# ALiBi attention: the distance bias of the diagonal blocks for heads 2 to 15 as factors on the exponentials, multiplied in by GpSimd, in place of TensorE products

## The reference, cut to what matters

```python
dist = jnp.abs(pos[:, None] - pos[None, :])
bias = -dist[None, :, :] * slopes[:, None, None]          # slopes = 0.5 ** head
scores = jnp.einsum('bhid,bhjd->bhij', q, k) / scale + bias
attn = jax.nn.softmax(scores, axis=-1)
out = jnp.einsum('bhij,bhjd->bhid', attn, v)
```

## Time and profile before

| | |
|---|---|
| time, median of 3 runs | 2564.29 us (2558.7 to 2565.91) |
| the profiled execution, its own time | 2567.91 us |
| its span in the trace | 2566.0 us |
| PE busy | 2248.5 us (88%) |
| DVE busy | 1718.1 us (67%) |
| ACT busy | 1463.6 us (57%) |
| POOL busy | 1089.2 us (42%) |
| granted TensorE clock, mean | 0.953 of full speed |

### The profile page before, as it was taken

One profiled execution on the slowest core, in us unless ns is written; L12 is line 12 of the kernel. 1 busy time (PEld: TensorE's weight loads), 2 busy tenths in 40 slices (PEclk: granted clock), 3 DMA queues, 4 the chain that ended last, 5 costly groups with the idle time before them and its releaser, 6 DMA issues. The chain is left out here.

```text
span 2566.0 us, 52577 instructions
## 1 busy us (share of the span) xinstructions
PE 2248.5 (88%) x21574; PEld 1674.9 (65%) x21574; DVE 1718.1 (67%) x2800; ACT 1463.6 (57%) x2382; POOL 1089.2 (42%) x800
## 2 busy tenths in 40 slices
PE   2799999999999779999879999999999985878476
PEld 1577777777777556666547777777777753766276
DVE  3677777777788457777467777778878845533554
ACT  0467676666666425555547767676666643435342
POOL 4655556555565100000065655556556505410432
PEclk8899999999999879999879999999999987999898
DMA  7000000099999300000000000000000012210013
GB/s 148 1 1 1 2 2 2 1 94 114 107 102 117 25 1 2 2 2 2 1 1 2 2 1 2 1 2 1 2 2 2 1 52 64 57 51 1 32 53 96
DMA packets 185425, 73.63 MB, mean 29 GB/s; under 512 B 79658, under 2 KB 181204, under 8 KB 185060
## 3 DMA queue, kind: packets, MB, share of 16 engines
q1 hardware_dynamic: 177172, 56.68, 19.0%
q0 software_dynamic: 5568, 10.12, 1.3%
q10 hardware_dynamic: 2448, 3.48, 0.6%
HBM read 24.05 MB, written 46.18 MB: 27 GB/s over the span
## 5 line engine op out<-in xcount | busy, mean ns | idle before, releaser
L467 POOL TENSOR_TENSOR work<-work,rot_tables 128x512 f32<-128x512 f32 x256 | 446.5, 1764 | 443.7 <-ACT work L566 443.7
L475 POOL TENSOR_TENSOR work<-work 128x1024 f32<-128x1024 f32 x128 | 305.1, 2383 | 13.0 <-DVE work L885 3.1
L885 DVE TENSOR_TENSOR work<-work,rot_tables 128x1024 f32<-128x1024 f32 x128 | 162.2, 1267 | 112.1 <-ACT work L566 112.1
L1042 DVE TENSOR_REDUCE small<-psum 128x4 f32<-128x1024 f32 x128 | 156.5, 1223 | 92.5 <-PE psum L1550 92.4
L1276 PE MATMUL psum<-qkv_w_hi,h_hi 128*128 128x512 f32 x384 | 182.6, 476 | 18.9 <-POOL h_lo L494 16.4
L1430 PE MATMUL psum<-centered,ffn_w 128*128 128x256 f32 x768 | 190.4, 399 | 6.1 <-DVE centered L946 2.9
L902 DVE TENSOR_TENSOR work<-work,small 128x1024 f32<-128x1024 f32 x128 | 159.5, 1248 | 51.2 <-ACT small L580 47.0
L677 ACT ACTIVATE work<-psum 128x1024 f32<-128x1024 f32 x128 | 131.2, 1025 | 102.3 <-PE psum L1557 102.3
L1368 PE MATMUL psum<-work 64*128 64x128 f32 (+1 forms) x2048 | 181.1, 307 | 0.0
L482 POOL TENSOR_TENSOR y_all<-centered,squared 64x256 f32<-64x256 f32 x64 | 48.5, 759 | 296.2 <-ACT squared L626 293.6
L1430 PEld LDWEIGHTS psum<-centered,ffn_w 128*128 128x128 f32 x768 | 145.8, 196 | 36.3 <-DVE centered L946 17.7
(11 more groups left out here) (280 smaller groups left out, 5561.5 us busy)
## 6 DMA issues: line engine op xcount, KB each, us to landing
h_area<-mean_weights SPq DMA_DIRECT2D x16, 2048.0 KB
tile_x<-h_area SPq DMA_DIRECT2D x78, 64.5 KB, 1.9
work<-y_tokens SPq DMA_DIRECT2D x8, 512.0 KB, 6.2
stage<-in_consts ACTq DMA_DIRECT2D x1, 3009.0 KB, 12.7
work<-in_x SPq DMA_DIRECT2D x4, 512.0 KB, 28.4
expert_w<-in_ew SPq DMA_DIRECT2D x1, 2048.0 KB, 8.5
expert_w<-in_ew SPq DMA_DIRECT2D x8, 256.0 KB, 6.8
out<-work SPq DMA_DIRECT2D x8, 256.0 KB, 3.5
```

The costliest lines, as they stand in the source:

```text
L467: last = pool.tensor_tensor(b[:, :, :, o_], a[:, :, :, i_], tab[:, l, 1, t, :, o_].unsqueeze(2).to_broadcast([P, 2, HEADS, 32]), ALU.mult)
L475: pool.tensor_tensor(rC[:, t, :], rC[:, t, :], rB[:, t, :], ALU.add).then_inc(f_sum, 1)
L885: dve.tensor_tensor(g(rC[:, t, :]), g(rA[:, t, :]), tab[:, l, 0, t, :, :].unsqueeze(2).to_broadcast([P, 2, HEADS, DH]), ALU.mult)\
L1042: dve.tensor_reduce(dst, PS[:, 0:2, :].rearrange("p b (t j) -> p b t j", t=TILES), AX, ALU.max, negate=True).then_inc(a_smax, 1)
```

## The change

For the pairs `r = 1` to `7` (heads 2 to 15) the four bias products behind the turned scores are gone; pair 0 keeps them, and the plain scores keep them for all pairs. In their place GpSimd multiplies the exponentials of the two diagonal blocks by exp(-2 * slope * relu(distance)), a product of 128 partitions by 512 elements in place in `PT4`, seven for each sequence (`far`). ScalarE makes the factors once, at the beginning of the layer, in the tile `y_all`, which the ffn stages use and which is free then: 14 activations of 128x256. `attend` now waits for GpSimd too (`a_f`), and on TensorE it is moved by one slot, from the odd to the even ones; `o_out` moves with it on ScalarE, from slots 3 and 7 to slots 4 and 0. `PT4` has three buffers in place of two. On GpSimd `split_h` is now written in the slot loop, in slot 5 behind that slot's `far`.

```diff
-        PT4 = [work[0][:, 2048 * n:2048 * (n + 1)].rearrange("p (h i) -> p h i", h=4) for n in range(2)]
+        PT4 = [work[0][:, 2048 * n:2048 * (n + 1)].rearrange("p (h i) -> p h i", h=4) for n in range(3)]
+        fac = Y[:, :, 1:T + 1].rearrange("p h (t i) -> p h t i", t=TILES)
...
+                def far(u):
+                    h, w = 2 * (u % 8), 2 * (u % 2)
+                    pool.wait_ge(a_p, u + 1)
+                    e = PT4[u // 2 % 3][:, w:w + 2, :].rearrange("p h (q i) -> p h q i", q=4)[:, :, 0:4:3, :]
+                    pool.tensor_tensor(e, e, fac[:, h:h + 2, :, :], ALU.mult).then_inc(a_f, 1)
+
+                pool.wait_ge(a_fac, 1)
+                for k in range(-2, SEQS + 4):
+                    for p in range(8):
+                        u = 8 * k + p - 11
+                        if 0 <= u < 8 * SEQS and u % 8:
+                            far(u)
+                        if p == 5 and k + 2 < SEQS:
+                            split_h(k + 2)
...
+                act.wait_ge(x_done, SEQS)
+                for h in range(2, AH):
+                    last = act.activation(fac[:, h, :, :], relub[:, :, :], ACT.Exp, scale=-2.0 * 0.5 ** h)
+                last.then_inc(a_fac, 1)
...
-                        if p == 3 and 0 <= k - 2 < SEQS:
+                        if p == 4 and 0 <= k - 2 < SEQS:
                             o_out(k - 2, 1)
-                        if p == 7 and 0 <= k - 1 < SEQS:
-                            o_out(k - 1, 0)
+                        if p == 0 and 0 <= k - 2 < SEQS:
+                            o_out(k - 2, 0)
...
+                    if turned and r > 0:
+                        far.then_inc(a_st, 1)
...
-                    if turned:
+                    if turned and r == 0:
...
                     pe.wait_ge(a_p, 2 * w + 2)
+                    pe.wait_ge(a_f, 7 * k + 2 * c + 1)
...
-                        if u % 2 == 0 and 0 <= (u - 2) // 2 < 4 * SEQS:
-                            attend((u - 2) // 2)
+                        if u % 2 == 1 and 0 <= (u - 3) // 2 < 4 * SEQS:
+                            attend((u - 3) // 2)
```

More of the change, by code:

```diff
@@ L305, in build @@
             ("zero", "mean", "centered", "squared", "var", "rstd", "normed", "h_split", "qk", "qk_hi", "qk_split")]
-        a_v, a_vs, a_s, a_smax, a_m, a_mT, a_madd, a_st, a_p, a_o, a_oTs = [sem(f"attn_{n}") for n in
-            ("v", "v_sb", "s", "s_max", "m_split", "mT", "m_added", "st", "p", "o", "oT_sb")]
+        a_v, a_vs, a_s, a_smax, a_m, a_mT, a_madd, a_st, a_p, a_f, a_fac, a_o, a_oTs = [sem(f"attn_{n}") for n in
+            ("v", "v_sb", "s", "s_max", "m_split", "mT", "m_added", "st", "p", "p_far", "factors", "o", "oT_sb")]
         a_rows, a_on, a_oT, a_ocs, a_proj = [sem(f"attn_{n}") for n in
@@ L514, in attn, with split_h @@
                     pool.memset(Vs[n][:, :, :, ADH:ADH + 1], 1.0).then_inc(a_zero, 1)
-                for n in range(SEQS):
+                def split_h(n):
                     pool.wait_ge(a_norm, n + 1)
@@ L676, in exps @@
                     act.wait_ge(a_st, u + 1)
-                    act.activation(PT4[u // 2 % 2][:, 2 * (u % 2):2 * (u % 2) + 2, :], PS[:, 4:6, :], ACT.Exp)\
+                    act.activation(PT4[u // 2 % 3][:, 2 * (u % 2):2 * (u % 2) + 2, :], PS[:, 4:6, :], ACT.Exp)\
                         .then_inc(a_p, 1)
@@ L1543, in scores @@
                             for b in range(2):
-                                pe.matmul(PS[:, 4 + b, t * T:(t + 1) * T], ks[m % 3][row(r, b), r // 2, t * P:(t + 1) * P],
-                                          qs[m % 3][row(r, b), r // 2, :], start=t == 0, stop=False, skip_group_check=True)
+                                far = pe.matmul(PS[:, 4 + b, t * T:(t + 1) * T], ks[m % 3][row(r, b), r // 2, t * P:(t + 1) * P],
+                                                qs[m % 3][row(r, b), r // 2, :], start=t == 0, stop=r > 0,
+                                                skip_group_check=True)
+                    if turned and r > 0:
+                        far.then_inc(a_st, 1)
                     if plain:
@@ L1569, in attend @@
                             last = pe.matmul(PS[SLOT * h:SLOT * (h + 1), 6, (c % 2) * T:(c % 2 + 1) * T],
-                                             Vs[k % 3][:, j, 4 * c + h, :], PT4[w % 2][:, h, j * T:(j + 1) * T],
+                                             Vs[k % 3][:, j, 4 * c + h, :], PT4[w % 3][:, h, j * T:(j + 1) * T],
                                              start=c % 2 == 0 and j == 0, stop=j == 1, skip_group_check=True)
```

## The result

The changed kernel takes 2596.06 us (median of 4 runs, 2594.89 to 2597.55) against 2562.82 us: a ratio of 1.0137, interval 1.0116 to 1.0158. It is 33 us slower, where 22 were forecast. The profiled execution took 2595.75 us with a span of 2593.9.

A forecast was written before the change was run, and what follows sets the result against it. TensorE was taken as the bound, busy 40.68 of 43 us, with VectorE's loop close behind. 20.4 + 1.3 + 0.3, +0.5 at the start, -0.5 at the end gave +22: 2590 profiled, 2586 median; own range 2574 to 2598.

The forecast's parts named there:

- a pitch of +2.4: Upper case per sequence, against +1.7 forecast: restarts behind the reduction at 0.14 us in place of 0.05.
- What is moved: `attend`, 1.00 us of TensorE, goes from odd slots to slots 0, 2, 4 and 6: +1.7 us, 23.1 us a sequence.
- the saving comes through: Rival, 11%: TensorE's work alone counts, 1.64 us a sequence saved, 2542 us; TensorE idle below 1 us a sequence.
- The loop over the reduction: Scores, VectorE's reduction, next scores: a slot cannot be shorter than this, 2.16 us, however little TensorE has to do.
- The restart of 0.05: TensorE starts the next scores 0.05 us after VectorE's reduction ends.
- give almost nothing: Removing the turned biases in a slot that a loop bounds: the slot goes from 2.26 to 2.16 us.
- What is added: GpSimd's products, taken at 1.4 us each, latency hidden; 14 activations for factors at the start, 0.5 us uncovered.
- Twelve sequences have the whole pattern: Sum over the layer: 12 x 1.7 = 20.4 us, plus 1.3 for the sequence ahead and 0.3 for the last.
- The end: End of the layer: ScalarE's loop gains 2 us, the last `attend` waits +1.2 to 1.8; taken as -0.5 us.
- The beginning: Start of the layer: the factors' activations, mostly beside GpSimd's memsets that hold back `center`; taken as 0.5 us.
- the first rival: 15%: TensorE's clock falls through gaps of 0.9 to 1.4 us in slots 1, 3, 5, 7; 2612 to 2640 us.
- the two heavy slots: Slots 6 and 0: at 1.2 GHz their 2.8 us would become 4 to 5, +2 to +4 a sequence.

The follow-up runs named there:

- The half reduction: The changed kernel with VectorE's reduction over every second key alone, 512 elements in place of 1024: 2568.87 us, ratio 1.0020.
- the filler: The changed kernel with 12 zero-weight TensorE products of 128x128, about 0.7 us, behind the scores of each odd slot: 2587.17 us, ratio 1.0092.
- filler on both sides: Besides the changed kernel, the kernel before with the zero-weight products in its first two iterations and alternate even slots of the drain: 2560.34 us, ratio 0.9992.

## Why the prediction was right

The direction and the mechanism of the steady stretch were right, and the sum was a third too small: 22 us where 33 were measured. That the time still lies within the forecast's own range, 2574 to 2598, is in part luck. Its upper end was made of a pitch of +2.4, products of 1764 ns and an uncovered start; the pitch used 0.2 of the 0.7 between +1.7 and +2.4, the other two did not come, and 9.5 us came from the clock and the ends of the layer, which the range did not hold.

- **What is moved.** The decisive step, +1.7 us a sequence, measured +1.89. Every slot came out within 0.04 us of its forecast: slots 0 and 1 5.24 (5.20), slot 2 4.29 (4.26), 3 2.27 (2.26), 4 4.30 (4.28), 5 2.16 (2.16), 6 2.79 (2.77), 7 2.20 (2.16). The moved `attend` is shown as the cause from both sides, by moving it alone and by moving it back. TensorE stands still for 8.72 of 47 us in the steady stretch, 4.3 a sequence, where the rival "the saving comes through" wanted less than 1.
- **The loop over the reduction.** The restart of 0.05 read off the slots without exponentials was right, and the trace of before, which named ScalarE in these slots, was no guide to what comes next. The half reduction and the left-out biases show it. That the biases "give almost nothing" in such a slot held: over all slots they give 0.48 a sequence of 1.6.
- **What is added.** GpSimd's product takes 1197 ns, nearly the lower of the two bounds, 1192; the sum took 1.4. No `attend` of the steady stretch waits for it. The factors take 4.39 us on ScalarE and lie beside the memsets, which hold back the first `center` for 4.05 as before: 0, where 0.5 was taken.
- **The mis-sized terms.** "Twelve sequences have the whole pattern" with the edges came to 22.0 for the 13 intervals, which measured 24.9. Of the 2.9 between them 12 x 0.19 = 2.3 is the pitch, and 0.6 the edge: the last interval grew by 2.2 (20.20 to 22.41), where 1.3 + 0.3 stood for the edges. The end was put at -0.5 and measured +4.4. The beginning, put at 0.5, measured +2.0, and two long intervals add 3.1. The end is the term that was most wrong, in size and in sign.
- **The clock.** The two long intervals, the beginning and part of the end are one thing, the first rival, which was given 15% as an alternative and came true in part beside the forecast. One of the prediction's own signs of being wrong, PEclk below 1.00 between 1000 and 1200 us, did appear: 0.66 in 1016.50 to 1021.50. It cost 1.6 us there, so it is the sign of the clock's part and not of the placement being wrong; slots 5 and 7 stayed above 2.1, and `attend` took 1.00 in slots 2 and 4. It did not hit the two heavy slots of each sequence, but slot 6 in two sequences of sixteen, the beginning, and the drain, where the prediction counted only that the slots get shorter. With the filler at the same pitch most of it is gone: the end from 48.67 to 40.92, the first `center` to the third `v_out` from 72.01 to 66.34. With filler on both sides the changed kernel's end is 1.7 us shorter than that of the kernel before (40.92 and 42.64), the sign that was forecast for it. The drain of before was at 0.86, and the changed kernel has still less to do there; the term for the end should have had that row in it. How the +4.4 of the end divides is not shown, though. The ends do not follow the clock alone: moving `attend` alone gave 49.19 us at 0.83, leaving the biases out 45.85 at 0.70, and `attend` one slot later 41.99 at 0.87. The page TensorE: Matmul & The Clock Gate of the Trainium skill, in "A second HAM failure mode: psum-queue depth-cycling", says that small idle gaps between groups of products make the clock swing. The trace agrees for the beginning and the drain. In the steady stretch, with gaps of up to 1.3 us in every second slot, it does so in two sequences of thirteen alone, so as a forecast for each sequence the rule would have been wrong.
- **What stays open.** Why just these two sequences, the same in the changed kernel and in the one without products, has not been told apart. Also open is why the layer's 5.7 us do not show in the time of the run with `attend` one slot later. The layer was read from the fastest execution of that kernel, outside the layer the profiled executions differ by some us (their times less the layer range from 2170.4 us, in the changed kernel, to 2179.0), and the loss at its second interval was seen in one trace only. Nor is it settled how much of the 33 us the clock costs: the filler brings back 8.9 by the medians and 16.6 in the layer of two single executions.

## What to carry to other kernels

Work is cheap or dear by its place: the same 1.0 us of products was free in a slot that waited for another engine anyway and cost its length in a full one, so before moving an instruction write down, slot by slot, the engine's own work beside the length of the loop that bounds the slot. When several loops end within a tenth of each other, the trace names the last, and taking that one away gains only the tenth; look for the next one in a stretch that lacks the first. And an engine that is unburdened without the pace rising has gaps, which can cost its clock: here zero products in the gaps gave 8.9 of the 33 us back, and 16.6 of the 34.5 in the layer of the profiled executions. Before a number is read from one trace, see where that execution lies among its kernel's times.

## What the hardware showed that was not expected

Short instructions of VectorE beside a GpSimd product ended only behind it in two places. `m_split`'s cast of 128x32 takes 0.24 us in the kernel before and without products on GpSimd, and 0.71 beside them (median of 16). The timeline of the changed kernel, first POOL, then DVE:

```profile
1115.55 1.09 POOL L528 TENSOR_TENSOR work<-work,y_all 128x512 f32<-128x512 f32 x1 [0.49 <-ACT work L693]
...
1116.02 0.71 DVE L1068 CAST work<-small 128x32 bf16<-128x32 f32 x1
```

The product ends at 1116.64, the cast 0.09 later. With the half reduction the times are shifted, the cast passes ahead of the product, and the difference behind it, with two inputs in SBUF, is caught instead, until 0.16 after the product's end; it takes 0.30 otherwise:

```profile
1120.66 1.09 POOL L528 TENSOR_TENSOR work<-work,y_all 128x512 f32<-128x512 f32 x1 [0.62 <-ACT work L693]
...
1120.60 0.24 DVE L1068 CAST work<-small 128x32 bf16<-128x32 f32 x1
1120.88 1.03 DVE L1069 TENSOR_TENSOR work<-small,work 128x32 bf16<-128x32 f32 x1
```

The reduction, which reads PSUM, kept its length beside GpSimd's products (1222 ns, and 1223 in the kernel before). The Trainium skill states in GPSIMD Engine Reference, "1. Specifications", that GpSimd shares its SBUF interfaces with VectorE and contends with instructions in a 2-port mode or with two inputs in SBUF. The measurement agrees for the difference, which has two inputs in SBUF; the cast has one, and no run here shows in which mode it ran. The price here is up to 0.7 us on an instruction of 0.3: the victim seems to wait to the end of the product. It cost the pitch nothing: without the products the sequence takes the same 23.26 us. Most of VectorE's work in this layer reads PSUM; where it does not, products on GpSimd may cost more.
